# A selective scan's preparation, worked in halves of the tokens

## The reference

```python
def ssm(x):                                  # x: (4, 256, 96)
    dbc = x @ x_proj_W.T                     # 6 + 16 + 16 columns
    delta = softplus(dbc[..., :6] @ dt_proj_W.T + dt_proj_b) * 0.001
    return selective_scan(x, delta, -exp(A_log), dbc[..., 6:22], dbc[..., 22:], D_param)

t = layer_norm(feat, ln_w, ln_b)             # over 256 channels, a second norm after the decoder's own
t = t @ in_proj_W.T                          # 256 -> 96 channels
t = conv1d(t, conv_w, conv_b)                # depthwise, 3 taps: the token before, this one, the one after
t = silu(t)                                  # t * sigmoid(t)
out = ssm(t) @ out_proj_W.T
```

## Time and profile before

| | us |
|---|---|
| median of 3 runs | 2822.2 (2821.17 to 2823.88) |
| the profiled execution | 2822.46 |
| its span, first to last instruction | 2820.6 |
| preparation block, first VectorE instruction to first of the next block | 467.7 to 535.2 |
| mean granted TensorE clock, share of full speed | 0.87 |

### The profile page before, as it was taken

How to read it: one execution, slowest core, us unless ns; L and a number is a source line. 1 busy time by engine, 2 the same in 40 slices (tenths; PEclk the granted TensorE clock), 3 DMA queues, 4 the chain that set the end, 5 groups by cost and what they waited for, 6 DMA issues and landing times. The chain is left out here.

```text
span 2820.6 us, 38166 instructions
## 1 busy us (share of the span) xinstructions
PE 2347.2 (83%) x14562; PEld 1556.1 (55%) x14562; DVE 1685.9 (60%) x3469; ACT 1029.1 (36%) x2400; POOL 768.8 (27%) x573
## 2 busy tenths in 40 slices
PE   6788353347999998978979798889998888999899
PEld 4546232115335555666868686745558665555555
DVE  5434987794346653386978788436656762666311
ACT  3023021571025551145546364435552042555211
POOL 1040001000019882210101000019880000988222
PEclk8779575558999998987979898899999968999999
DMA  1010000003000001040101011120001003000411
GB/s 36 10 31 1 23 1 15 6 1 112 1 0 1 1 1 61 12 156 16 46 16 46 16 35 27 34 71 1 1 1 45 22 4 102 1 1 1 124 45 35
DMA packets 100526, 81.78 MB, mean 29 GB/s; under 512 B 52704, under 2 KB 91856, under 8 KB 99769
## 3 DMA queue, kind: packets, MB, share of 16 engines
q1 hardware_dynamic: 99321, 77.89, 9.6%
q0 software_dynamic: 1024, 1.45, 0.2%
HBM read 73.58 MB, written 5.35 MB: 28 GB/s over the span
## 5 line engine op out<-in xcount | busy, mean ns | idle before, releaser
L2032 POOL TENSOR_SCALAR work<-work,small 128x512 f32<-128x512 f32 x384 | 593.4, 1562 | 669.1 <-DVE small L1965 669.1
L1960 DVE TENSOR_REDUCE small<-psum 128x2 f32<-128x1024 f32 x192 | 234.7, 1224 | 176.2 <-PE psum L1910 176.2
L2008 ACT ACTIVATE work<-psum,small 128x512 f32<-128x512 f32 x384 | 259.8, 684 | 123.1 <-DVE small L1960 123.1
L1920 PEld LDWEIGHTS psum<-consts,work 128*128 128x128 f32 x1536 | 165.6, 142 | 114.2 <-POOL work L2032 99.7
L1910 PE MATMUL psum<-keysT,arena_a 64*128 64x512 f32 x768 | 219.4, 650 | 8.7 <-ACT work L2008 5.8
L1920 PE MATMUL psum<-consts,work 128*128 128x128 f32 x1536 | 211.6, 281 | 3.8 <-DVE work L1971 2.6
L1932 PE MATMUL psum<-work,keys 128*64 128x256 f32 x1536 | 186.9, 385 | 0.0
L2015 ACT ACTIVATE work<-psum 128x512 f32<-128x512 f32 x192 | 114.7, 597 | 161.8 <-PE psum L1920 161.8
L1932 PEld LDWEIGHTS psum<-work,keys 128*64 128x64 f32 x1536 | 101.7, 136 | 111.8 <-issue 68.0
L2878 PE MATMUL psum<-xnT,arena_a 128*128 128x256 f32 x512 | 134.6, 417 | 13.8 <-DVE arena_b L3329 11.8
L1971 DVE COPY work<-psum 128x512 f32<-128x512 f32 x192 | 130.8, 681 | 18.9 <-PE psum L1920 18.6
(11 more groups left out here) (585 smaller groups left out, 4731.0 us busy)
## 6 DMA issues: line engine op xcount, KB each, us to landing
arena_b<-alpha_rows SPq DMA_DIRECT2D x16, 512.0 KB, 6.2
arena_a<-in_L_xattn_Wo SPq DMA_DIRECT2D x3, 2048.0 KB, 13.7
arena_a<-in_L_xattn_Wq SPq DMA_DIRECT2D x3, 2048.0 KB, 12.8
arena_a<-in_L_xattn_w_kc_q SPq DMA_DIRECT2D x3, 1536.0 KB, 12.4
arena_a<-in_L_attn_w_qkv SPq DMA_DIRECT2D x1, 4096.0 KB
arena_a<-in_L_xattn_W_qr SPq DMA_DIRECT2D x3, 768.0 KB
arena_b<-in_L_ffn_w_fc SPq DMA_DIRECT2D x1, 2048.0 KB
arena_b<-in_L_ffn_w_proj SPq DMA_DIRECT2D x1, 2048.0 KB
```

Of the source, the lines that this page charges most:

```text
L1920: mm = nc.tensor.transpose(ps[:, 4 + j, c * P:(c + 1) * P], probs[u % NPB][:, j, c * P:(c + 1) * P], k.c["ident"])
L1960: nc.vector.tensor_reduce(top[:, 2 * u:2 * u + 2], ps[:, u % 2 * 2:u % 2 * 2 + 2, :], AX.X, ALU.max, negate=True).then_inc(*maxed.up())
L2008: nc.scalar.activation(probs[u % NPB][:, j, :], ps[:, u % 2 * 2 + j, :], ACT.Exp, bias=top[:, i:i + 1], accum_out=total[:, i:i + 1]).then_ ...
L2032: nc.gpsimd.tensor_scalar(probs[u % NPB][:, j, :], probs[u % NPB][:, j, :], total[:, i:i + 1], None, ALU.mult).then_inc(*scaled.up())
```

## The change

- VectorE signals `ln_xn` after each of the 8 tiles. TensorE transposes tile by tile and steps `turned` after 4 and after 8 tiles. Evacuation, input projection, convolution, tanh, `u`, the low-rank projection and `low` go by halves of 512 tokens, each with a semaphore step of its own (`taken`, `proj`, `conved`, `tanhed`, `silued`, `low` are now stepped once per half).
- The factor 0.5 of the gate goes into the convolution: `conv_w` and `conv_b` are scaled by 0.5 (two instructions of VectorE on 96x3 and 96x1), tanh takes `conv` with no scale, and `u = u * 0.5` is gone.
- GpSimd waits for `ln_xn` of the eighth tile before it rotates the keys.
- The skip goes to ScalarE (three copies with a scale, once the 12 DMAs have landed), `delta`'s factor 0.001 too; `du` is one instruction on the unscaled sum, `(mag * 0.001) * own_u`. A new step `summed` lets ScalarE and VectorE work on that sum at the same time.
- The DMAs of sequences 0 and 1 wait for the first half of `u` only.

```diff
             k.link(dve, nc.vector.scalar_tensor_tensor(out=rs[:, 1, :], in0=mv[:, :, 0], scalar=-1.0, in1=rs[:, 0, :],
                                                        op0=ALU.mult, op1=ALU.mult), "dve")
             for t in range(NT):
-                last = nc.vector.tensor_scalar(xn2[:, t, :], xn[:, t, :], rs[:, 0, t:t + 1], rs[:, 1, t:t + 1],
-                                               ALU.mult, ALU.add)
-            last.then_inc(*k.sig("ln_xn").up())
+                nc.vector.tensor_scalar(xn2[:, t, :], xn[:, t, :], rs[:, 0, t:t + 1], rs[:, 1, t:t + 1],
+                                        ALU.mult, ALU.add).then_inc(*k.sig("ln_xn").up())
             k.wait_weights(dve, "first")
-            for i in range(4):
-                dve.wait_ge(*turned.at(1))
-                c, g = divmod(i, 2)
-                last = nc.vector.tensor_scalar(xn2T[:, c, g * 512:(g + 1) * 512], ps[:, i, :], ln_w[:, c:c + 1],
-                                               ln_b[:, c:c + 1], ALU.mult, ALU.add)
-            last.then_inc(*taken.up())
-
-            dve.wait_ge(*proj.at(1))
-            src = ps[0:C, 4:6, :].rearrange("p a (b s) -> p (a b) s", b=2)
-            cv = conv.rearrange("p (b s) -> p b s", b=B)
-            k.link(dve, nc.vector.tensor_scalar(cv, src, conv_w[:, 1:2], conv_b[:, 0:1], ALU.mult, ALU.add), "dve")
-            k.link(dve, nc.vector.scalar_tensor_tensor(out=cv[:, :, 1:S], in0=src[:, :, 0:S - 1], scalar=conv_w[:, 0:1],
-                                                       in1=cv[:, :, 1:S], op0=ALU.mult, op1=ALU.add), "dve")
-            nc.vector.scalar_tensor_tensor(out=cv[:, :, 0:S - 1], in0=src[:, :, 1:S], scalar=conv_w[:, 2:3],
-                                           in1=cv[:, :, 0:S - 1], op0=ALU.mult, op1=ALU.add).then_inc(*conved.up())
-
-            dve.wait_ge(*conved.at(1))
-            dve.wait_ge(*k.sig("tanhed").at(1))
-            k.link(dve, nc.vector.scalar_tensor_tensor(out=u, in0=u, scalar=1.0, in1=conv, op0=ALU.add,
-                                                       op1=ALU.mult), "dve")
-            nc.vector.tensor_scalar(u, u, 0.5, None, ALU.mult).then_inc(*silued.up())
-            dve.wait_ge(*silued.at(1))
-            dve.wait_ge(*proj.at(2))
-            nc.vector.tensor_copy(low.rearrange("p (a b) -> p a b", a=2), ps[0:R, 6:8, :]).then_inc(*lowed.up())
-
-            dve.wait_ge(*proj.at(3))
+            nc.vector.tensor_scalar(conv_w, conv_w, 0.5, None, ALU.mult)
+            k.link(dve, nc.vector.tensor_scalar(conv_b, conv_b, 0.5, None, ALU.mult), "dve")
+            for g in range(2):
+                dve.wait_ge(*turned.at(g + 1))
+                for c in range(2):
+                    last = nc.vector.tensor_scalar(xn2T[:, c, g * 512:(g + 1) * 512], ps[:, 2 * c + g, :], ln_w[:, c:c + 1],
+                                                   ln_b[:, c:c + 1], ALU.mult, ALU.add)
+                last.then_inc(*taken.up())
+
+            for g in range(2):
+                dve.wait_ge(*proj.at(g + 1))
+                src = ps[0:C, 4 + g, :].rearrange("p (b s) -> p b s", b=2)
+                cv = conv[:, g * 512:(g + 1) * 512].rearrange("p (b s) -> p b s", b=2)
+                k.link(dve, nc.vector.tensor_scalar(cv, src, conv_w[:, 1:2], conv_b[:, 0:1], ALU.mult, ALU.add), "dve")
+                k.link(dve, nc.vector.scalar_tensor_tensor(out=cv[:, :, 1:S], in0=src[:, :, 0:S - 1], scalar=conv_w[:, 0:1],
+                                                           in1=cv[:, :, 1:S], op0=ALU.mult, op1=ALU.add), "dve")
+                nc.vector.scalar_tensor_tensor(out=cv[:, :, 0:S - 1], in0=src[:, :, 1:S], scalar=conv_w[:, 2:3],
+                                               in1=cv[:, :, 0:S - 1], op0=ALU.mult, op1=ALU.add).then_inc(*conved.up())
+            dve.wait_ge(*conved.at(2))
+            for g in range(2):
+                own = slice(g * 512, (g + 1) * 512)
+                dve.wait_ge(*k.sig("tanhed").at(g + 1))
+                nc.vector.scalar_tensor_tensor(out=u[:, own], in0=u[:, own], scalar=1.0, in1=conv[:, own], op0=ALU.add,
+                                               op1=ALU.mult).then_inc(*silued.up())
+            for g in range(2):
+                dve.wait_ge(*proj.at(g + 3))
+                nc.vector.tensor_copy(low[:, g * 512:(g + 1) * 512], ps[0:R, 6 + g, :]).then_inc(*lowed.up())
+
+            dve.wait_ge(*proj.at(5))
             for j in range(J):
                 last = nc.vector.tensor_scalar(z[:, j, :], ps[:, j // 2, j % 2 * S:(j % 2 + 1) * S], dt_b[:, j:j + 1], None, ALU.add)
             last.then_inc(*k.sig("z").up())
@@ -1434,17 +1436,15 @@
             k.link(dve, refine_exp(k, dve, a_exp, a_log, 1.0, a_ln), "dve")
             k.link(dve, nc.vector.tensor_scalar(a_log, a_exp, -1.0, None, ALU.mult), "dve")
             log1p_tail(k, dve, e, h[0], h[1], mag)
-            k.link(dve, nc.vector.tensor_tensor(delta, delta, mag, ALU.add), "dve")
-            k.link(dve, nc.vector.tensor_scalar(delta, delta, 0.001, None, ALU.mult), "dve")
+            nc.vector.tensor_tensor(mag, delta, mag, ALU.add).then_inc(*k.sig("summed").up())
+            dve.wait_ge(*k.sig("summed").at(1))
             dve.wait_ge(*laned.at(16 * B * J))
-            nc.vector.tensor_tensor(du, delta, own_u, ALU.mult)
-            for j in range(J):
-                nc.vector.tensor_scalar(hC[1][:, j, :], own_u[:, j, :], skip[:, j:j + 1], None, ALU.mult)
+            nc.vector.scalar_tensor_tensor(out=du, in0=mag, scalar=0.001, in1=own_u, op0=ALU.mult, op1=ALU.mult)
 
         @block.sync
         def _(sp):
-            sp.wait_ge(*silued.at(1))
             for b in range(B):
+                sp.wait_ge(*silued.at(b // 2 + 1))
                 for j in range(J):
                     sp.dma_start(own_u[lane(b), j, :], u[G * j:G * j + G, b * S:(b + 1) * S]).then_inc(*laned.up(16))
 
@@ -1452,8 +1452,10 @@
         def _(act):
             act.wait_ge(*var.at(1))
             nc.scalar.activation(rs[:, 0, :], mv[:, :, 1], ACT.Sqrt, bias=EPSC).then_inc(*std.up())
-            act.wait_ge(*conved.at(1))
-            nc.scalar.activation(u, conv, ACT.Tanh, scale=0.5).then_inc(*k.sig("tanhed").up())
+            for g in range(2):
+                own = slice(g * 512, (g + 1) * 512)
+                act.wait_ge(*conved.at(g + 1))
+                nc.scalar.activation(u[:, own], conv[:, own], ACT.Tanh).then_inc(*k.sig("tanhed").up())
             context_keep(k, act)
             act.wait_ge(*k.sig("z").at(1))
             k.link(act, nc.scalar.activation(mag, z, ACT.Abs), "act")
@@ -1461,27 +1463,33 @@
             k.link(act, nc.scalar.activation(a_exp, a_log, ACT.Exp), "act")
             nc.scalar.activation(dBu[0], e, ACT.Ln, bias=k.c["tiny"])
             nc.scalar.activation(a_ln, a_exp, ACT.Ln, bias=k.c["tiny"]).then_inc(*spin.up())
+            act.wait_ge(*laned.at(16 * B * J))
+            for j in range(J):
+                nc.scalar.activation(hC[1][:, j, :], own_u[:, j, :], ACT.Copy, scale=skip[:, j:j + 1])
+            act.wait_ge(*k.sig("summed").at(1))
+            nc.scalar.activation(delta, mag, ACT.Copy, scale=0.001)
 
         @block.tensor
         def _(pe):
-            pe.wait_ge(*k.sig("ln_xn").at(1))
             for t in range(NT):
+                pe.wait_ge(*k.sig("ln_xn").at(t + 1))
                 for c in range(2):
                     mm = nc.tensor.transpose(ps[:, 2 * c + t // 4, t % 4 * P:(t % 4 + 1) * P],
                                              xn2[:, t, c * P:(c + 1) * P], k.c["ident"])
-            mm.then_inc(*turned.up())
-            pe.wait_ge(*taken.at(1))
+                if t % 4 == 3:
+                    mm.then_inc(*turned.up())
             for n in range(2):
+                pe.wait_ge(*taken.at(n + 1))
                 for c in range(2):
                     mm = nc.tensor.matmul(ps[0:C, 4 + n, :], w_in[:, c, :], xn2T[:, c, n * 512:(n + 1) * 512],
                                           start=c == 0, stop=c == 1)
-            mm.then_inc(*proj.up())
+                mm.then_inc(*proj.up())
             context_turn(k, pe)
-            pe.wait_ge(*silued.at(1))
             for n in range(2):
+                pe.wait_ge(*silued.at(n + 1))
                 mm = nc.tensor.matmul(ps[0:R, 6 + n, :], w_x[:, 0:R], u[:, n * 512:(n + 1) * 512], start=True, stop=True)
-            mm.then_inc(*proj.up())
-            pe.wait_ge(*lowed.at(1))
+                mm.then_inc(*proj.up())
+            pe.wait_ge(*lowed.at(2))
             pe.wait_ge(*k.sig("keys_kept").at(1))
             for j in range(J):
                 for b in range(B):
@@ -1491,6 +1499,7 @@
 
         @block.gpsimd
         def _(pool):
+            pool.wait_ge(*k.sig("ln_xn").at(NT))
             context_rotate(k, pool)
```

## The result

| | before | changed |
|---|---|---|
| median of 6 runs of each (lowest to highest), us | 2821.8 (2821.2 to 2824.2) | 2800.6 (2796.5 to 2806.7) |
| ratio | | 0.9925, interval 0.9915 to 0.9936 |
| profiled execution, us | 2822.46 | 2796.49 |
| its span, us | 2820.6 | 2794.7 |
| block: first VectorE instruction (L1384) to the next block's first on ScalarE, us | 67.55 | 51.03 |

A forecast was written before the change was run, and what follows sets the result against it. No engine was taken as full up to `z`: one chain where engines take turns. 13.3 us to `z` plus 1.4 at the block's end made 14.7, from 2822.2 to 2807.5 us; range 2804.5 to 2812.5.

The forecast's parts named there:

- Refinement and tiles: Block's start: with GpSimd's rotation later, refinement gives back 1.77 us and the eight tiles 2.73.
- Evacuations, projection, convolution: By halves: evacuations 0.74 us each, projection 2.6 per half, convolution 4.6 for both; first half of `u` at 486.35, second 487.0.
- The two scalings: VectorE's scalings of the convolution's weights, between tiles and evacuations: 0.7 us for both, bounds 0.4 and 1.2.
- The chain that ends last: Before `z`: keys rotated at 484.4, turned by TensorE until 486.4, copied by ScalarE until 490.2; `low` 490.75; gain 13.3 us.
- TensorE's clock behind the turns: Low-rank projection left at 0.50 of full speed, 3.58 us; at 1.00, with the last matmuls, up to 2 us more.
- The end of the block: After `z`: `du` starts where `delta`'s scaling did, ScalarE's copies hidden; gain 1.4 us, at worst 1.0.
- How the runs differ: 1.1 us added to the 16.6 us upper gain to set the range's lower end, 2804.5.
- B: Rival: TensorE's clock at 0.50 for the turns of the keys; gain 12.8 us, 2809.4; chance 0.24.
- C: Rival: VectorE waits behind GpSimd instruction by instruction beside the moved rotation, 7.7 us; gain 7.1, 2815.1; chance 0.07.
- D: Rival: GpSimd's rotation itself is stretched, doubled to 17.1 us; gain 4.3, 2817.9, no difference; chance 0.04.
- E: Rival: the long tiles have another cause than GpSimd; tiles end at 480.27, gain 10.3 us, 2811.9; chance 0.06.
- F: Rival: slower through TensorE's clock in later stages, about 12 us per point, two points 2831; chance 0.03.

The follow-up runs named there:

- factor_back: Changed kernel with the factor 0.5 as a product on each half of `u` again, none in the weights: `z` at 25.72 us, its one run 2811.5 us.

## Why the prediction was wrong, point by point

- **Refinement and tiles, 4.5 us**: right, 1.77 and 2.73, and shown by the two experiments on GpSimd's wait.
- **Evacuations, projection, convolution**: convolution's halves at 4.6 us were right (471.48 to 476.12). The two scalings took 0.2 in all, not 0.7: they were all but done when GpSimd's first instruction began, so whether they would have waited for one wasn't put to the test. The input projection ended 14.3 us into the block, not 15.6, and TensorE then idled 2.44 us ahead of the turns where about 1 was named as the sign; the clock stayed at 1.00 all the same. `u` was ready at 18.0 and 18.6 (18.7 and 19.3 forecast).
- **The chain that ends last, up to the turns and the copies**: right. Turns 16.72 us into the block (16.7 to 16.8 forecast), copies done at 22.45 (22.5).
- **TensorE's clock behind the turns**: the step of the sum that failed. "The low-rank projection ran at 0.50 and I leave it there." It ran at 1.00, as did the matmuls for `z`: 1.88 and 1.50 us, not 3.58 and 2.78. That put the copies of the keys last, not `low`, and `z` at 24.15, not 25.97: 15.1 us gained where the term said 13.3. The text had this as its bound, 15.2. A clock that falls after idleness is part of what a shorter chain changes, and should have been in the sum.
- **The end of the block, 1.4 us**: right.
- **The kernel before**: one profile was taken for its block. Two more had 69.35 and 68.06, not 67.55. The mean gain of the block is 17.3, so 0.8 us of it were in the base.
- **How the runs differ, 1.1 us**: the step of the range that failed, and the larger one. The block gained 16.5 us by the two first profiles, which the range held; the medians differ by 21.3. Of the 6.9 us between 2807.5 and 2800.6 the clock is 1.8 and the block's base 0.8. Another 1.0 is the start of the sum: 2822.2 from three runs, where 85 runs of the kernel before have their median at 2821.2. The last 3.2 are how the changed kernel's six runs fell: 2800.6, where its 18 runs have 2803.8 (still 0.7 under the range). That is chance as far as the runs show it, and it isn't one stage's: layer 0 varies by 9 us and the rest of the span by 6 in profiles of the same kernel. The 1.1 us came from three runs that agreed within 2.7; 85 runs go from 2814.5 to 2829.1.
- **Rivals**: B did happen, in factor_back, for one execution. C and D fell: the convolution's instructions beside the rotation took 0.74 to 0.81, the rotation 8.5. The Trainium skill (GPSIMD Engine Reference, Specifications) names VectorE instructions with two SBUF inputs as one of two kinds that contend with GpSimd; none of these neighbours has two, and the trace agrees. E fell by the tiles. Of F the mechanism is real (unchanged stages last longer or shorter with the matmuls in them), but without a direction.

What decides whether the clock rises or falls at a given place, when the same instructions run again, isn't settled; I ran nothing that sets it.

## What to carry to other kernels

Look for one instruction of a group that is many times its median, and for the engine that was busy for just that time; moving the other work gave back 4.5 us here, though it put that work on the chain. In a chain of hand-overs, halves pay well beyond their fixed costs: 10.5 us (3 to 4 of them by the clock) for 0.7 of VectorE. And where short bursts of TensorE set the time, price both clock levels, and take the spread of whole runs from many of them before a range is drawn.

## What was not expected of the hardware

- Executions of one program differ by 9 us in layer 0 (437.1 to 446.1 before, 436.6 to 444.7 changed) and by 6 in the rest of the span. In one stage of 624 matmuls that no edit touches, TensorE was busy 104.5 us of 128.0 at a mean clock of 0.77, and 98.1 of 118.7 at 0.83.
- After 3.77 us of idleness the clock stood at 1.00 in one execution and at 0.50 in the other.
- A VectorE tile of 128x256 beside GpSimd's addition took 2495 ns in two different kernels, and 403 to 412 ns in the changed kernel, without it; VectorE's arithmetic on 8 columns (L189 to L193 and L1393) took 0.37 to 0.64 us beside the rotation, and 0.17 without it.
